# Self-attention's softmax denominators: TensorE sums every tile of each head group's first chunk, and three tiles of the fourth chunk in place of four

## The reference, cut to what matters

```python
qkv = x @ Wqkv.T
dots = jnp.einsum('bhid,bhjd->bhij', q, k) * scale
dots = jnp.where(causal_mask, -jnp.inf, dots)
attn = jax.nn.softmax(dots, axis=-1)
out = jnp.einsum('bhij,bhjd->bhid', attn, v)
```

## Time and profile before

| | |
|---|---|
| median of 3 executions | 2617.73 us (2617.07 to 2618.23) |
| the profiled execution | 2619.38 us |
| its span, first to last instruction | 2617.6 us |
| TensorE busy | 2421.4 us, 93% |
| VectorE busy | 1718.9 us, 66% |
| ScalarE busy | 1102.5 us, 42% |
| GpSimd busy | 1118.5 us, 43% |

### The profile page before, as it was taken

The page is one execution under the profiler, slowest core; times in us unless marked ns, Lnnn a source line. Parts: engine busy times, 40 slices in busy tenths (PEclk is TensorE's granted clock), DMA queues, the critical chain, the costliest instruction groups (busy, mean ns, idle before and its releaser), DMA issues. The chain is left out here.

```text
span 2617.6 us, 36273 instructions
## 1 busy us (share of the span) xinstructions
PE 2421.4 (93%) x13556; PEld 1013.8 (39%) x13556; DVE 1718.9 (66%) x3957; ACT 1102.5 (42%) x2066; POOL 1118.5 (43%) x404
## 2 busy tenths in 40 slices
PE   7999799999999999989946799999999999999998
PEld 3444223333323232323214354454445444454543
DVE  5433687777767677767405577767677776767665
ACT  4331156666666666666623242332324232322320
POOL 0000379989898989898952111102111211101100
PEclk9999799999999999999977899999999999999999
DMA  7864312212121213040021101010100101010000
GB/s 254 298 206 156 92 38 54 58 42 58 42 63 37 71 33 86 14 118 16 24 104 50 45 1 62 1 46 17 40 22 1 62 1 46 17 46 17 1 17 17
DMA packets 130443, 155.00 MB, mean 59 GB/s; under 512 B 19838, under 2 KB 98174, under 8 KB 129245
## 3 DMA queue, kind: packets, MB, share of 16 engines
q1 hardware_dynamic: 130269, 152.69, 19.1%
HBM read 99.96 MB, written 52.17 MB: 58 GB/s over the span
## 5 line engine op out<-in xcount | busy, mean ns | idle before, releaser
L762 ACT ACTIVATE probs<-st_ps 128x512 f32<-128x512 f32 (+3 forms) x1280 | 610.2, 535 | 339.9 <-PE st_ps L865 194.4
L637 POOL TENSOR_TENSOR total<-total,probs 128x2048 f32<-128x2048 f32 (+3 forms) x200 | 706.2, 3531 | 77.2 <-ACT probs L762 58.6
L804 DVE TENSOR_REDUCE seg_max<-s_ps 128x1 f32<-128x512 f32 x768 | 505.9, 685 | 139.2 <-PE s_ps L851 137.0
L865 PE MATMUL st_ps<-q_pair,k_pair 98*128 98x512 f16 (+3 forms) x1280 | 445.2, 362 | 34.9 <-ACT probs L762 28.8
L851 PE MATMUL s_ps<-k_pair,q_pair 96*128 96x512 f16 (+3 forms) x1280 | 446.1, 364 | 33.1 <-DVE seg_max L804 11.6
L1429 PE MATMUL fps<-x2T,w_p_hi 128*128 128x512 f16 x1024 | 317.3, 379 | 0.0
L885 PE MATMUL o_ps<-probs,v_sb 128*32 128x512 f32 (+3 forms) x2560 | 307.2, 553 | 0.0
L808 DVE CUSTOM_DVE_ANT_0 s_ps<-s_ps,later 128x384 f32<-128x384 f32 (+3 forms) x512 | 250.7, 497 | 85.8 <-issue 82.4
L1429 PE MATMUL fps<-w_p_hi,hT 128*128 128x512 f16 x1024 | 305.9, 380 | 0.0
L865 PEld LDWEIGHTS st_ps<-q_pair,k_pair 98*128 98x128 f16 x1280 | 125.0, 99 | 345.3 <-ACT probs L762 244.8
L1133 POOL TENSOR_TENSOR rstd<-rstd,keep_power 128x4 f32<-128x4 f32 x24 | 26.0, 1085 | 542.0 <-DVE rstd L1254 542.0
(11 more groups left out here) (164 smaller groups left out, 3403.5 us busy)
## 6 DMA issues: line engine op xcount, KB each, us to landing
k_pair<-k_parts SPq DMA_DIRECT2D x96, 128.0 KB, 3.9
q_pair<-q_parts SPq DMA_DIRECT2D x96, 128.0 KB, 4.9
x_raw<-xT_in SPq DMA_DIRECT2D x8, 1024.0 KB, 6.1
q_parts<-qk_out SPq DMA_DIRECT2D x32, 256.0 KB, 3.7
k_parts<-qk_out SPq DMA_DIRECT2D x32, 256.0 KB, 3.8
piece_raw<-w_in SPq DMA_DIRECT2D x8, 1024.0 KB, 8.7
v_rows<-v_out SPq DMA_DIRECT2D x32, 256.0 KB, 2.1
w_parts<-piece_cut SPq DMA_DIRECT2D x8, 1024.0 KB, 5.6
```

The costliest lines, as they stand in the source:

```text
L637: last = nc.gpsimd.tensor_tensor(summed[:, :, off:], other[:, :, off:], probs[:, k % NP, :, off:], ALU.add)
L762: nc.scalar.activation(probs[:, k % NP, h, off:], st_ps[:, p % (2 * NVU) % RING, off:], ACT.Exp, scale=SCALE).then_inc(exp_done.sem, 1)
L804: nc.vector.reduce_max(highest, s_ps[:, slot], AX.X).then_inc(s_read.sem, 1)
L865: last = nc.tensor.matmul(st_ps[:, slot, off:], k_pair[a][:, h, kt * P:(kt + 1) * P], q_pair[a][:, c, h, off:], start=True, stop=not diagonal)
```

## The change

`SUMMED` names the tiles that TensorE sums itself: all four of c0, kt 2 of c1, kt 2 and 5 of c2 (as before), and kt 3, 7 and 11 of c3 (before 2, 5, 8 and 11). `POOLED` is what is left. So c0 has no adds and no total any more; c3 has one more add and one sum less. The sums of c0 are made at lags of their own (`FIRST_SUMS` = 12, 10, 8, 6 for kt 0 to 3), which puts them at steps 15, 17, 19 and 21 of the group; the total of c0 had been at step 27. A sum reads and writes only the columns from `off` on, so those of c0 are 512, 384, 256 and 128 wide. The buffers of `total` alternate over the three chunks that have one (`total_of`). ScalarE learns that the outputs of c0 are whole from a new semaphore, `first_ready`, and that its denominators are from `pv_done` of its last tile.

```diff
-    POOLED = [[n for n, (k, kt) in enumerate(KU) if k == c and (kt >= c * TT or kt % 3 != 2)]
-              for c in range(CPB)]
+    SUMMED = [(0, 1, 2, 3), (2,), (2, 5), (3, 7, 11)]
+    POOLED = [[n for n, (k, kt) in enumerate(KU) if k == c and kt not in SUMMED[c]] for c in range(CPB)]
+    TOTALLED = CPB - 1
...
+    FIRST_SUMS = 12, 10, 8, 6
...
+    def total_of(c):
+
+        return c // CPB * TOTALLED + c % CPB - 1
...
-                    summed = total[:, c % 2]
+                    t = total_of(k // NKU * CPB + c)
+                    summed = total[:, t % 2]
                     if starts:
 
-                        pool.wait_ge(den_ready.sem, den_ready.at(i, k // NKU * CPB + c - 2))
+                        pool.wait_ge(den_ready.sem, den_ready.at(i, t - 2))
...
-                    act.wait_ge(pv_done.sem, pv_done.at(i, c // CPB * NKU + LAST_TILE[c % CPB]))
+                    if c % CPB == 0:
+                        act.wait_ge(first_ready.sem, first_ready.at(i, c // CPB))
+                    else:
+                        act.wait_ge(pv_done.sem, pv_done.at(i, c // CPB * NKU + LAST_TILE[c % CPB]))
...
-                    act.wait_ge(den_ready.sem, den_ready.at(i, c))
+                    if c % CPB == 0:
+                        act.wait_ge(pv_done.sem, pv_done.at(i, c // CPB * NKU + LAST_TILE[0]))
+                    else:
+                        act.wait_ge(den_ready.sem, den_ready.at(i, total_of(c)))
...
                 if k % NKU in POOLED[c]:
                     last.then_inc(pv_done.sem, 1)
+                elif final:
+                    last.then_inc(first_ready.sem, 1)
...
-                opens = all(n in POOLED[c] for n, (x, _) in enumerate(KU) if x == c and n < k % NKU)
+                opens, closes = kt == SUMMED[c][0], k % NKU == LAST_TILE[c]
+                off = max(kt - c * TT, 0) * P
...
-                    last = nc.tensor.matmul(den_ps[out, :], ones[:], probs[:, k % NP, h], start=opens, stop=False)
+                    last = nc.tensor.matmul(den_ps[out, off:], ones[:], probs[:, k % NP, h, off:], start=opens,
+                                            stop=closes)
...
-                opens = all(n in POOLED[c % CPB] for n, (x, _) in enumerate(KU) if x == c % CPB)
-                if opens:
-                    pe.wait_ge(den_taken.sem, den_taken.at(i, c - 1))
+                t = total_of(c)
...
-                    last = nc.tensor.matmul(den_ps[out, :], ones[:], total[:, c % 2, h], start=opens, stop=True)
+                    last = nc.tensor.matmul(den_ps[out, :], ones[:], total[:, t % 2, h], start=False, stop=True)
...
+                for kt, lag in enumerate(FIRST_SUMS):
+                    k = tile_at(s, lag, first, end)
+                    if k is not None and KU[k % NKU] == (0, kt):
+                        sums(i, k)
                 k = tile_at(s, SUMS, first, end)
-                if k is not None:
+                if k is not None and KU[k % NKU][0] > 0:
                     sums(i, k)
                 c = chunk_at(s, TOTALS, first, end)
-                if c is not None:
+                if c is not None and c % CPB > 0:
                     totals(i, c)
```

More of the change, by code:

```diff
@@ L580, in self_attention @@
         pv_done = Count(nc, stack, "pv_done", 2 * NKU)
-        den_ready = Count(nc, stack, "den_ready", 2 * CPB)
+        den_ready = Count(nc, stack, "den_ready", 2 * TOTALLED)
+        first_ready = Count(nc, stack, "first_ready", 2)
         o_taken = Count(nc, stack, "o_taken", 2 * CPB)
@@ L830, in _ @@
         def _(pe):
-            for count in (st_ready, pv_done, den_ready, s_ready):
+            for count in (st_ready, pv_done, den_ready, first_ready, s_ready):
                 count.lead(pe)
```

## The result

The changed kernel takes 2632.28 us (median of 5 executions, 2630.42 to 2637.72) against 2617.73 us before (5 executions, 2616.26 to 2622.35): a ratio of 1.0058, 95% interval 1.0044 to 1.0071. The change costs 0.6%, where 0.4% (2629 us, range 2618 to 2637) was forecast. The profiled execution is the fastest of the five: 2630.42 us, span 2628.6, so 11.0 us more span than before. The size of the cost is uncertain by some 2 us: 28 further executions of the kernel before, made beside the experiments, have a median of 2620.1 us, and from there the cost is 12.2 us.

The account below looks back on a forecast made before the run. TensorE was taken to bound c0, c1 and c3, GpSimd's backlog c2 and group 7's end. Terms 12.2 - 2.7 + 4.6 - 3.0 = +11.1 us took the median from 2617.73 to 2628.8, forecast 2629 us, range 2618 to 2637.

Parts of the forecast that it names:

- What bounds which stretch: TensorE bounds c0, c1 and c3; GpSimd's backlog in c2 costs some 8 us in each of groups 1 to 5.
- the prediction's own signs of being wrong: L777 no longer waits for L647, groups' length does not grow by 1.6 us, or low stretches all of one kind.
- c0, +1.74 us in seven groups: TensorE in c0: four sums cost 2.59 us, the total that goes saves 0.85; seven groups give +12.2 us.
- Group 0, put at nothing: c0 of group 0: TensorE has room beside busy VectorE, so the added 1.7 us cost nothing (bounds 0 to 1.7).
- c3, 0.1 us left of 1.08: Groups 1 to 5: c3's total waits for GpSimd, leaving -0.1 us each; groups 0 and 6 -1.1 each; sum -2.7 us.
- The end, +4.6: Group 7: one more add in GpSimd's row without pause makes the last total 4.64 us later, hidden by nothing.
- The new stall in c3 of group 7: ScalarE's wait in c3 for L647 of c2: in time by 1.5 us, except in group 7, where it doesn't matter.
- The low clock, -3 us: Half clock after c2's stall in groups 1 to 5: one or two become short, some 2.6 us each (bounds -13, +3).
- the short kind of 3.4 us: Group 0's low-clock length, against 10.2 us in groups 1 to 5; expected in one or two of those five.
- The first (low clock, no change): Rival: short low clock in all or most groups, giving 2619 us, no change; chance 0.12.
- the third (a fall of the clock at the new wait): Rival: TensorE's 1 us wait before c3's total lowers the clock at five boundaries, +8.5 us, 2637 us; chance 0.10.
- The second, GpSimd's relief reaching the stall: Rival: removing c0's adds brings L647 forward, ending c2's stall and low clock, 2589 us; chance 0.06.

Follow-up runs that it names:

- The kernel with the third sum in c2: Kernel before with one more TensorE sum in c2 (kt 2, 5 and 8) and one GpSimd add less: 2575.48 us, ratio 0.9827.
- the run of c0 alone: Changed kernel with c3's sums as before (kt 2, 5, 8 and 11): 2631.43 us, ratio 1.0038 to the kernel before.
- c3 alone: Kernel before with three sums in c3 (kt 3, 7 and 11) in place of four, c0 as before: 2623.43 us, ratio 1.0015.
- the three kernels with the third sum in c2: Sums kt 2, 5 and 8 in c2: on the kernel before 2575.48 us, on the changed kernel 2590.16, on the kernel before with all sums behind values 2574.50.
- the ten with narrow adds: Kernel before with three sums in c3, GpSimd's adds of kt 13, 14 and 15 of c3 cut to 16 columns: 2613.46 us, ratio 0.9973.

## Why the prediction was right, point by point

**What bounds which stretch: right.** Adds of c0 lie in GpSimd's idle time (10.16 us of it now), the stall in c2 kept its length, and the time of c0 and c3 is TensorE's. The kernel with the third sum in c2 supports this from the other side: the same account of stall and low clock gave 42 us less, and 44.7 us less were measured. One of the prediction's own signs of being wrong did come, though: the length of a group was to grow by 1.6 us, and groups 1, 2, 3 and 5 grew by only 0.2 to 0.8 us. Kt 3 of c1 is late by the full amount in them (2.32 us, of which 0.79 us is the wait at the total); what they regain they regain behind the stall, where their low stretch is shorter. Group 4, which kept 10.2 us, grew by 1.8.

**c0, +1.74 us in seven groups: right in kind, 0.2 us too much.** The four sums cost what was computed. The difference is at the total that went: from kt 2 to kt 3 of c1 the changed kernel takes 20.69 - 18.09 = 2.60 us, the one before 18.37 - 14.76 = 3.61, so it gains 1.0 us and not 0.85. Why the total cost more than its columns there the runs don't show. The term is 7 x 1.53 = 10.7, not 12.2. Group 0, put at nothing, has kt 3 of c1 0.6 us earlier than before. The rule of the Trainium skill, TensorEngine Tiling (Array Packing), Instruction Overhead, was rightly not taken: by it this term would have been an estimated 3 us higher, and the four sums take 2.62 us together, where the rows gave 2.59.

**c3, 0.1 us left of 1.08: right, by two errors that cancel.** The row of adds from kt 4 on was computed as 42.0 us long (793.8 to 835.8) and took 42.1 us. The total waits 0.75 us, not 0.9, and the sum that went was worth about 0.85 us, not 1.08; so 0.1 us or less is left. Group 0 was expected to have no such wait and has it (0.58 us of idle time at the start of group 1); group 6 has none, as expected. Six boundaries spend 0.79 us and seven groups save 0.85, so the term is about -1.2, not -2.7. That this error and the one in c0's term, each 1.5 us, cancel is luck.

**The end, +4.6: right.** Group 7 takes 6.17 us more: 1.53 in c0 and 4.64 for one add in a row without pause. The new stall in c3 of group 7 was foreseen too: ScalarE waits 4.70 us there for the scaling of c2, and it costs nothing, since the last total waits 10.33 us anyway.

**The low clock, -3 us: right in sign, wrong in how it comes about.** The place of the fall did move and the lengths did change, but to 6.8 us, and in group 0 to 10.2, neither of which I had; the short kind of 3.4 us did not appear in groups 1 to 5. And I priced lengths. What costs is TensorE's busy time in them, and the long stretches before lay partly over the stall: 47.37 us busy before and 44.22 after, 3.2 us less, 1.6 us at half clock. The lengths of the groups say the same. Without the low clock each of groups 1 to 6 should grow by 1.53 + 0.79 - 0.85 = 1.47 us. Against that groups 1 to 5 come out 3.8 us shorter in sum, but group 0, which I had left out, loses 1.7 us to its longer stretch and group 6, where one grew from 3.4 to 6.8 us, 0.6 us. So in the profiled execution the term is an estimated -1.5 us. What it is in the median the runs don't show: the two medians of the kernel before alone, 2617.73 and 2620.1 us, lie further apart than that.

**The sum.** With the terms as measured, 10.7 - 0.6 - 1.2 + 4.6 - 1.5 is 12.0 us; the last total starts 12.4 us later, 0.3 of it from before group 0. The forecast median, 2629 us, is 3.3 us under the measured one; 1.5 us of that can be the low clock, and the rest is within what the medians leave open.

**The rivals.** The first (low clock, no change) and the third (a fall of the clock at the new wait) did not come: the clock is at 1.00 through the waits of 0.75 us. The third was nearer than its argument had it, which took 2.5 us for the shortest stall with a fall behind it: waits of 1.06 to 1.38 us for VectorE had one in three of the experiments. The second, GpSimd's relief reaching the stall, fell with the unchanged 49.0 us and the run of c0 alone.

## What to carry to other kernels

Work taken from an engine counts only where somebody waits for that engine: GpSimd was busy eight or nine tenths of most slices, yet its adds in c0 were worth nothing, and one add less in c2 of each group, though TensorE had to take it over, was worth 45 us. Follow the row of work back from the wait that somebody has to the last idle time in it; only what lies between counts. And where an engine is in time by less than a piece of work is long, taking that piece from its partner buys a wait.

## What the runs showed of the hardware

I had not expected how loosely the low clock follows its cause. Stalls of TensorE of 3.8 us were followed by 6.8 or 10.2 us at half clock, and stalls of 2.3 to 2.6 us in group 0 by 3.4 us (the kernel before), 6.8 (c0 alone) or 10.2 (after, c3 alone), with nearly the same work around them. Waits of 0.4 to 1.35 us at the totals were followed by none, but waits of 1.29, 1.38 and 1.06 us for a maximum of VectorE in c3 were followed by 3.4 us at half clock, in one group each of the three kernels with the third sum in c2. So in these runs the length of a wait alone does not tell whether the clock falls.

The executions of one kernel differ along with the clock. In the 15 of the kernel before beside the first experiments, those with a mean granted clock of 0.958 average 2621.3 us and those with 0.961 average 2617.0 us; in the ten with narrow adds the clock goes from 0.957 to 0.962 and the time from 2616.5 to 2609.5 us. Executions of a kernel without the stall in c2 spread over 1.7, 2.3 and 3.8 us (4 each), those of the kernel before over 5.7 us in 15; four executions are few, so that the missing low stretches are the reason is my reading, not shown.
